# Scores of two attention stages: three split fp32r products against one plain fp32 product

## What is computed

```python
def _L0_xattn_ref(x, y, ...):                       # first layer
    xn = layernorm(x, ln1_w, ln1_b)
    yn = layernorm(y, ln2_w, ln2_b)
    q = (xn @ Wq), k, v = (yn @ Wkv)                # split into 16 heads of 16
    attn = jax.nn.softmax(jnp.einsum('bhqd,bhkd->bhqk', q, k) * scale, axis=-1)
    o = jnp.einsum('bhqk,bhkd->bhqd', attn, v).transpose(0, 2, 1, 3).reshape(B, N1, C1)
    x = x + (o @ Wproj + bproj)
    h = jax.nn.gelu(layernorm(x, ln3_w, ln3_b) @ W1 + b1, approximate=False)
    return x + (h @ W2 + b2)

def _L1_xattn_ref(x, encoder_out, norm_w, wq, wkv, wout):   # second layer
    xn = x * jax.lax.rsqrt(jnp.mean(x * x, axis=-1, keepdims=True) + EPS_RMS) * norm_w
    q, k, v = ...                                   # q and k turned by rope, then scaled to length 1 per head
    logits = jnp.einsum('bqhd,bkhd->bhqk', q, k) * scale
    out = jnp.einsum('bhqk,bkhd->bqhd', jax.nn.softmax(logits, axis=-1), v)
    return residual + out @ wout
```

## Time and profile before

| what | us |
|---|---|
| time before, median of 3 runs | 385.97 |
| lowest and highest of them | 385.35, 391.71 |
| the profiled execution: its span | 386.9 |
| its own time apart from the span | not given |
| TensorE busy, share | 356.5, 92% |
| VectorE busy, share | 294.4, 76% |
| ScalarE busy, share | 239.3, 62% |
| GpSimd busy, share | 197.1, 51% |

### The profile page before, as it was taken

The page is one execution under the profiler, slowest core; times in us unless marked ns, Lnnn a source line. Parts: engine busy times, 40 slices in busy tenths (PEclk is TensorE's granted clock), DMA queues, the critical chain, the costliest instruction groups (busy, mean ns, idle before and its releaser), DMA issues.

```text
span 386.9 us, 11499 instructions
## 1 busy us (share of the span) xinstructions
PE 356.5 (92%) x4475; PEld 318.7 (82%) x4475; DVE 294.4 (76%) x654; ACT 239.3 (62%) x464; POOL 197.1 (51%) x177
## 2 busy tenths in 40 slices
PE   8998999999999989898999999978889989989974
PEld 5977888888888867798999998978778878878854
DVE  4799987989899773267755559467899999999752
ACT  2356677666677655815644476163877777777862
POOL 2474544554665611003331233248899998999810
PEclk9999999999999999999999999999999999999999
DMA  6853001110000000000000000000001001010001
GB/s 157 246 158 121 27 25 43 32 28 25 2 3 4 22 2 2 2 2 0 0 0 0 0 0 3 10 22 0 22 12 36 26 26 42 29 37 14 29 30 41
DMA packets 14432, 12.39 MB, mean 32 GB/s; under 512 B 2996, under 2 KB 13752, under 8 KB 14392
## 3 DMA queue, kind: packets, MB, share of 16 engines
q1 hardware_dynamic: 14384, 11.83, 10.4%
q10 hardware_dynamic: 8, 0.00, 0.0%
HBM read 9.73 MB, written 2.10 MB: 31 GB/s over the span
## 4 chain that ended last, share of the span: by engine, by line
PE 58%; issue 22%; DVE 10%; ACT 5%; POOL 4%; POOLq 0%; DVEq 0%; ACTq 0%
PE bank_qk L697 9%; PE banks_s L745 6%; PE bank_y L834 4%; PE bank_y L828 3%; PE banks_s L1032 3%; PE bank_t L800 3%; PE bank_qk L722 3%; PE bank_o L736 3%; PE bank_t L697 3%; PE bank_qk L726 3%; DVE row_max L1203 2%; POOL x_all L375 2%; PE bank_y L1052 2%; PE bank_o L1021 2%; PE bank_y L929 1%
## 5 line engine op out<-in xcount | busy, mean ns | idle before, releaser
L413 POOL TENSOR_TENSOR norm_inv<-norm_sq_min,minus_half 128x32 f32<-128x32 f32 x16 | 87.5, 5468 | 1.8 <-DVE norm_sq_min L1374 1.8
L576 ACT ACTIVATE W_s<-banks_s,b_cols 128x256 f32<-128x256 f32 x60 | 25.0, 469 | 41.3 <-PE banks_s L915 41.3
L342 POOL TENSOR_TENSOR masked<-qkT_r,halves_t 128x512 fp32r<-128x512 f32 x32 | 32.9, 1050 | 24.1 <-DVE qkT_r L1193 24.1
L477 ACT ACTIVATE PT<-banks_s 128x1024 f32<-128x1024 f32 x32 | 31.0, 1022 | 20.3 <-PE banks_s L782 18.3
L1203 DVE TENSOR_REDUCE row_max<-banks_s 128x8 f32<-128x1024 f32 x32 | 37.6, 1218 | 7.7 <-PE banks_s L745 7.7
L368 POOL TENSOR_TENSOR b_var_eps<-b_mean_var,eps_t 128x2 f32<-128x2 f32 x8 | 1.6, 197 | 69.1 <-DVE b_mean_var L1137 69.1
L915 PE MATMUL banks_s<-lnT_hi,W_hi 128*128 128x256 f32 x120 | 34.2, 285 | 0.0
L915 PE MATMUL banks_s<-lnT_hi,W_lo 128*128 128x256 f32 x120 | 33.9, 283 | 0.0
L915 PE MATMUL banks_s<-lnT_lo,W_hi 128*128 128x256 f32 x120 | 33.9, 283 | 0.0
L642 ACT ACTIVATE PT<-banks_s 128x1024 f32<-128x1024 f32 x32 | 31.1, 1024 | 4.1 <-PE banks_s L1032 4.1
L745 PE MATMUL banks_s<-masked,qkT_r 32*128 32x256 f32 x768 | 31.5, 294 | 1.6 <-DVE row_max L1203 1.3
(11 more groups left out here) (171 smaller groups left out, 1095.6 us busy)
## 6 DMA issues: line engine op xcount, KB each, us to landing
ctx_in<-in_ctx SPq DMA_DIRECT2D x32, 96.0 KB, 2.0
x_all<-in_x SPq DMA_DIRECT2D x16, 128.0 KB, 2.1
W_s<-in_L_xattn_W SPq DMA_DIRECT2D x2, 1024.0 KB, 6.4
out<-Wq_s SPq DMA_DIRECT2D x16, 128.0 KB, 1.8
Wq_s<-in_L_xattn_Wq SPq DMA_DIRECT2D x1, 256.0 KB, 3.0
Wkv_s<-in_L_xattn_Wkv SPq DMA_DIRECT2D x1, 256.0 KB, 3.2
Wproj_s<-in_L_xattn_Wproj SPq DMA_DIRECT2D x1, 256.0 KB, 4.2
wout_s<-in_L_xattn_wout SPq DMA_DIRECT2D x1, 256.0 KB, 3.0
```

The source lines that it names most:

```text
L342: nc.gpsimd.tensor_tensor(masked[:, r, 1, :, half, :], qkT_r[:, r, 1, :, :].bitcast(fp32), ones, ALU.mult)\
L413: nc.gpsimd.tensor_tensor(norm_inv[:, j, :], norm_sq_min[:, j, :], minus_half[:, :], ALU.pow)\
L477: nc.scalar.activation(PT[:, 2 * h:2 * h + 2, :], banks_s[:, 2 * h:2 * h + 2, :], ACT.Exp, scale=HD ** -0.5)\
L576: last = nc.scalar.activation(hT[:, m, :], (bank or bank_s[u])[:, 256 * k:256 * k + 256], ACT.Gelu, bias=b1_cols[:, m:m + 1])
```

## The change

The score products of both attentions become plain fp32 matmuls of unsplit operands: 8 products a set in place of 24. `qkT_r` becomes `qkT` (fp32, no high and low), `masked` loses its axis of 2 too.

In stage A ScalarE copies the queries and keys once (`queries_keys_T`, the former L446), its `masked_hi` goes, VectorE's `queries_keys_lo` goes, and GpSimd makes the two masked copies from ScalarE's copy (`masked_pool`), in the place of `masked_lo`. In stage C ScalarE's three copies stay (`units_out`, now fp32), and VectorE's `units_lo` goes. What waited for VectorE's low parts now waits for ScalarE's copies. The projections, the products with `picks_wide` and those of stages B and C (`split_mm`) stay as they are.

```diff
-        qkT_r = sb("qkT_r", 128, RING, 2, 4, TOK, dtype=fp32r)
-        masked = sb("masked", 128, RING, 2, 4, 2, TOK, dtype=fp32r)
-        pair = masked[:, :, :, 0:KT, :, :]
+        qkT = sb("qkT", 128, RING, 4, TOK)
+        masked = sb("masked", 128, RING, 4, 2, TOK)
+        pair = masked[:, :, 0:KT, :, :]
...
-            def masked_lo(t):
+            def masked_pool(t):
 
                 if ok(t):
                     r = t % RING
-                    pool.wait_ge(a_qk_lo, t + 1)
+                    pool.wait_ge(a_qk_ready, t + 1)
                     wait(pool, a_shifted, t - 2)
                     for half in range(2):
                         ones = halves_t[:, half:half + 1].unsqueeze(2).broadcast_to([128, 4, TOK])
-                        nc.gpsimd.tensor_tensor(masked[:, r, 1, :, half, :], qkT_r[:, r, 1, :, :].bitcast(fp32), ones, ALU.mult)\
-                            .then_inc(a_masked_lo, 1)
+                        nc.gpsimd.tensor_tensor(masked[:, r, :, half, :], qkT[:, r, :, :], ones, ALU.mult).then_inc(a_masked_pool, 1)
...
-            def queries_keys_hi(t):
+            def queries_keys_T(t):
 
                 if ok(t):
                     act.wait_ge(A["qk_mm"], t + 1)
                     wait(act, a_shifted, t - 2)
-                    nc.scalar.activation(qkT_r[:, t % RING, 0, :, :], bank_qk[:, :].rearrange("p (a b) -> p a b", a=4), ACT.Copy)\
-                        .then_inc(a_qk_hi, 1)
-
-            def masked_hi(t):
-
-                if ok(t):
-                    act.wait_ge(a_qk_hi, t + 1)
-                    for half in range(2):
-                        nc.scalar.activation(masked[:, t % RING, 0, :, half, :], qkT_r[:, t % RING, 0, :, :].bitcast(fp32),
-                                             ACT.Copy, scale=halves_t[:, half:half + 1]).then_inc(a_masked_hi, 1)
...
                 exps_a(s - 4)
-                queries_keys_hi(s - 1)
+                queries_keys_T(s - 1)
                 on_T(s - 5)
-                masked_hi(s - 1)
                 out_T(s - 4)
...
-            def units_hi(t, j):
+            def units_out(t, j):
 
                 if ok(t):
                     act.wait_ge(c_turned, t + 1)
                     wait(act, C["scores"], NG * (t - 1))
                     for half in range(2):
-                        nc.scalar.activation(pair[:, j, 0, :, half, :], bank_o[:, 0:C1].rearrange("p (a b) -> p a b", a=KT),
-                                             ACT.Copy, scale=halves_t[:, half:half + 1]).then_inc(c_unit_hi, 1)
-                    nc.scalar.activation(qkT_r[:, j, 0, KT:, :], bank_o[:, C1:].rearrange("p (a b) -> p a b", a=KT), ACT.Copy)\
-                        .then_inc(c_unit_hi, 1)
+                        nc.scalar.activation(pair[:, j, :, half, :], bank_o[:, 0:C1].rearrange("p (a b) -> p a b", a=KT),
+                                             ACT.Copy, scale=halves_t[:, half:half + 1]).then_inc(c_unit_T, 1)
+                    nc.scalar.activation(qkT[:, j, KT:, :], bank_o[:, C1:].rearrange("p (a b) -> p a b", a=KT), ACT.Copy)\
+                        .then_inc(c_unit_T, 1)
...
-                    for n, (a, b) in enumerate(HI_LO):
-                        for g in range(QUARTERS):
-                            last = mm(bank_s[g][:, 2 * TOK * tile:2 * TOK * (tile + 1)], qkT_r[quad(g), r, a, rows + tile, :],
-                                      masked[quad(g), r, b, columns + tile, :, :], start=n == 0 and (stop or tile == 0), stop=stop and n == 2)
-                            if stop and tile == KT - 1 and n == 2:
-                                last.then_inc(A["scores"], 1)
+                    for g in range(QUARTERS):
+                        last = mm(bank_s[g][:, 2 * TOK * tile:2 * TOK * (tile + 1)], qkT[quad(g), r, rows + tile, :],
+                                  masked[quad(g), r, columns + tile, :, :], start=stop or tile == 0, stop=stop)
+                        if stop and tile == KT - 1:
+                            last.then_inc(A["scores"], 1)
 
             def scores_a(t):
 
                 if ok(t):
-                    pe.wait_ge(a_masked_hi, 2 * t + 2)
-                    pe.wait_ge(a_masked_lo, 2 * t + 2)
+                    pe.wait_ge(a_masked_pool, 2 * t + 2)
...
-                    wait(pe, c_unit_lo, t)
+                    wait(pe, c_unit_T, 3 * t)
...
-                    pe.wait_ge(c_unit_lo, t + 1)
+                    pe.wait_ge(c_unit_T, 3 * t + 3)
                     wait(pe, C["exped"], 2 * t)
                     for half in range(KT):
-                        for n, (k, q) in enumerate(HI_LO):
-                            for g in range(NG):
-                                last = mm(bank_s[g][:, 2 * TOK * half:2 * TOK * (half + 1)], qkT_r[quad(g), j, k, KT + half, :],
-                                          pair[quad(g), j, q, half, :, :], start=n == 0, stop=n == 2)
-                                if half == KT - 1 and n == 2:
-                                    last.then_inc(C["scores"], 1)
+                        for g in range(NG):
+                            last = mm(bank_s[g][:, 2 * TOK * half:2 * TOK * (half + 1)], qkT[quad(g), j, KT + half, :],
+                                      pair[quad(g), j, half, :, :], start=True, stop=True)
+                            if half == KT - 1:
+                                last.then_inc(C["scores"], 1)
...
-                    pe.wait_ge(c_unit_lo, upto(t + 3))
+                    pe.wait_ge(c_unit_T, 3 * upto(t + 3))
...
-            def queries_keys_lo(t):
-
-                if ok(t):
-                    r = t % RING
-                    dve.wait_ge(a_qk_hi, t + 1)
-                    v.tensor_tensor(qkT_r[:, r, 1, :, :], bank_qk[:, :].rearrange("p (a b) -> p a b", a=4),
-                                    qkT_r[:, r, 0, :, :].bitcast(fp32), ALU.subtract).then_inc(a_qk_lo, 1)
...
                 norm(s)
-                queries_keys_lo(s - 1)
                 maxima(s - 2)
...
-            def units_lo(t, j):
-
-                if ok(t):
-                    dve.wait_ge(c_unit_hi, 3 * t + 3)
-                    for half in range(2):
-                        v.scalar_tensor_tensor(pair[:, j, 1, :, half, :], bank_o[:, 0:C1].rearrange("p (a b) -> p a b", a=KT),
-                                               halves_t[:, half:half + 1], pair[:, j, 0, :, half, :].bitcast(fp32),
-                                               ALU.mult, ALU.subtract)
-                    v.tensor_tensor(qkT_r[:, j, 1, KT:, :], bank_o[:, C1:].rearrange("p (a b) -> p a b", a=KT),
-                                    qkT_r[:, j, 0, KT:, :].bitcast(fp32), ALU.subtract).then_inc(c_unit_lo, 1)
...
                 turned(s - 1, 1 - j)
-                units_lo(s - 3, 1 - j)
                 square_sums(s - 1, 1 - j)
```

More of the change, by code:

```diff
@@ L201, in build @@
         A, C = att_sems("a"), att_sems("c")
-        a_centred, a_qk_hi, a_qk_lo, a_masked_hi, a_masked_lo = (
-            sem(f"a_{k}") for k in ("centred", "qk_hi", "qk_lo", "masked_hi", "masked_lo"))
+        a_centred, a_qk_ready, a_masked_pool = (sem(f"a_{k}") for k in ("centred", "qk_ready", "masked_pool"))
         a_maxed, a_max_hi, a_max_lo, a_max_turned, a_maxT, a_shifted = (
@@ L208, in build @@
         c_stored = [sem(f"c_stored{j}") for j in range(2)]
-        c_rope, c_turned, c_rot, c_rot_sq, c_norm_sq, c_norm_min, c_norm_inv, c_unit, c_unit_hi, c_unit_lo = (
-            sem(f"c_{k}") for k in ("rope", "turned", "rot", "rot_sq", "norm_sq", "norm_min", "norm_inv", "unit", "unit_hi", "unit_lo"))
+        c_rope, c_turned, c_rot, c_rot_sq, c_norm_sq, c_norm_min, c_norm_inv, c_unit, c_unit_T = (
+            sem(f"c_{k}") for k in ("rope", "turned", "rot", "rot_sq", "norm_sq", "norm_min", "norm_inv", "unit", "unit_T"))
         b_stats_raw, b_stats, b_var, b_rstd, b_norm, b_bias, b_T, b_lnT_hi, b_lnT_lo, b_w1, b_gelu, b_hT_hi, b_hT_lo, b_w2, b_x, b_raw, b_centred = (
@@ L347, in step_a @@
                 residual_bias(s)
-                masked_lo(s - 1)
+                masked_pool(s - 1)
             pool.wait_ge(const_ready, 2)
@@ L355, in _ @@
             inverse_std(2)
-            masked_lo(0)
+            masked_pool(0)
             residual_bias(1)
@@ L359, in _ @@
             inverse_std(3)
-            masked_lo(1)
+            masked_pool(1)
             residual_bias(3)
-            masked_lo(2)
+            masked_pool(2)
             inverse_std(4)
             residual_bias(4)
-            masked_lo(3)
+            masked_pool(3)
             def inverse_std_b(p):
@@ L445, in queries_keys_hi @@
                     wait(act, a_shifted, t - 2)
-                    nc.scalar.activation(qkT_r[:, t % RING, 0, :, :], bank_qk[:, :].rearrange("p (a b) -> p a b", a=4), ACT.Copy)\
-                        .then_inc(a_qk_hi, 1)
-            def masked_hi(t):
-                if ok(t):
-                    act.wait_ge(a_qk_hi, t + 1)
-                    for half in range(2):
```

(28 more changed lines are left out.)

## The result

The changed kernel took 394.51 us (391.67 to 395.81, four runs) against 387.32 us (385.35 to 391.71, four runs) for the kernel before: a ratio of 1.0202, 95% interval 1.0135 to 1.027. With the same program run again (first experiment) the ratio is 1.0124 (1.0061 to 1.0188). It is slower, by one to two per cent; the forecast was 1.1%. The ratios leave out executions more than 1.5% above the fastest of the same kernel, so they are not the quotients of the medians shown. Experiment 1 shows what the two ratios have in them besides the change.

A forecast was written before the change was run, and what follows sets the result against it. TensorE was taken to bound the steady part of both attention stages. Opening -0.7, first stage +3.9, passage -0.35, second stage +1.65, end -0.2 sum to +4.3 us: forecast 390.3 us, 1.1% slower, range 385 to 397 us.

The forecast's parts named there:

- A burst: Score products on TensorE, both attention stages: 1.07 us for a set instead of 0.92, 0.15 us more.
- edge: Part of each score burst outside its rounds (first weights, draining): 0.20 us, the same before and after.
- Bursts on the path: Score bursts that lengthen the run: 26 in the first attention stage, +3.9 us; 11 in the steady second, +1.65 us.
- The passage: Into the second attention stage, where VectorE's low parts leave the chain: 0.35 us gained, from 0 to 0.5.
- The end: Last two score bursts of the second stage: a 0.25 us wait goes, each burst 0.15 longer, -0.2 us together.
- the opening: 13 to 40.5 us, VectorE on the path: without its low-part subtraction, work comes sooner, -0.7 us including five bursts.
- the move costs nothing: First stage: GpSimd's two masked products start one step sooner, their result wanted some 6 us later, so no cost.
- The base: Starting time: the profiled 386.9 us span taken as 0.9 us above the run median 385.97, turning 391.2 into 390.3.
- two abreast: Rival: product halves run in program order, 2.14 us a burst, +1.22 on 39 bursts, about 436 us; chance 0.07.
- staggered loads: Rival: weight loads of 128 columns stagger the strips, +0.48 us a burst on 39 bursts, about 404 us; chance 0.08.
- single streaming: Rival: a 32-row strip pays no second streaming, burst 0.68 us, about 374 us, faster; chance 0.04.
- More relief than counted: Rival: freed VectorE and ScalarE time is worth more, in second-stage tiles and opening, about 386 us; chance 0.06.

The follow-up runs named there:

- first experiment: The changed kernel with no edit, timed in more rounds beside the kernel before: 394.01 us (six runs), ratio 1.0124.
- Experiment 1: The same as the first experiment: the changed kernel again with no edit, more rounds: 394.01 us (six runs), ratio 1.0124.
- run 5: The changed kernel with score loops swapped in both attention stages, so each strip's products follow one another in the program: 397.14 us, one run.
- run 3: The kernel before with plain fp32 score products in the second attention stage alone: 387.04 us, ratio 0.9987.
- run 2: The changed kernel, but the second attention stage keeps the split products and VectorE's low parts: 392.66 us, ratio 1.0084.
- run 4: The changed kernel, but GpSimd's masked copies of tile 2 wait until VectorE has normalised tile 3: 393.42 us, ratio 1.0105.
- run 8: The changed kernel, but ScalarE makes both masked copies of the first stage and GpSimd none: 391.23 us (four runs), ratio 1.0117.
- run 6: The changed kernel with each score product of the second stage made twice into the same bank: 403.84 us, one run.
- runs 5 and 7: 7: the kernel before with only the high x high product in second-stage scores, VectorE still making low parts: 387.81 us, one run.

## Why the prediction was right, and where it was not

The forecast was slower by 4.3 us, within 2%; it is 5.14 us from the first burst on. Step by step:

- **A burst.** Forecast 1.07 us, 16 instructions of 0.216 us in four rounds and 0.20 us of edge; the chain has 1.07 to 1.08, and 1.94 when doubled. Reading four abreast from the starts of L800 was right, and program order falls with run 5. The mean of one is 400 ns, not near 380. The trace has the four first ones of a burst at 478 ns, each starting together with its own weight load, and the other twelve at 374. The starts also show what the edge is: rounds start at 0, 0.32, 0.54 and 0.75 us and the next line at 1.07, so the first and the last step are 0.10 us longer each. The split bursts have the same 0.10 us twice.
- **Bursts on the path.** Forecast 26 in the first stage, +3.9; +4.01. In the second 11, +1.65; ten tiles gave +1.60 and the eleventh burst 0.16 more. Tiles of 8.6 and 7.4 us: 8.65 and 7.44.
- **The passage.** -0.35 forecast, -0.33 measured. The chain there:

```profile
274.52 0.64 ACT rot_sq L601
275.19 0.70 DVE norm_sq L1341
...
276.00 0.70 DVE inT_r L1317
```

The 1.1 us of L1389 and L1392 are gone, and ScalarE's squares end last in their place, which is why only a third of it came back. From x_all the passage is the same in run 3 (4.95 us) and untouched in run 2 (5.28).
- **The end.** -0.2 forecast for the last two bursts; the stretch from burst 13 gave -0.36, with +0.16 for the thirteenth burst in it, so about -0.5. The waits of 0.25 us went, as said, but TensorE's turn of the values, which waited, went from 0.41 to 0.22 us too, and that I had not counted. The kernel before has, behind the wait of 0.25 us at 368.53,

```profile
368.78 0.41 PE bank_o L1062 x2
369.19 1.01 PE banks_s L1032 x23
```

and the changed kernel

```profile
374.21 0.91 PE bank_qk L682 x6
375.12 0.22 PE bank_o L1044 x2
375.34 1.20 PE banks_s L1014 x16
```

Each time 0.44 us goes and the burst is 0.19 longer: -0.5 for two.
- **The step that went wrong: the opening.** "The third maxima and the work up to 40.5 us come 0.7 us sooner." It came 0.25 us later. The relief that I summed was there: run 4, which only removes the collision, has -0.54. What I left out is in my sentence that GpSimd's products start one step sooner and "the move costs nothing". I asked only who waits for their result, not whom they run beside. Taking L1193 out took away the wait that kept GpSimd apart from VectorE's L1185. In the steady part such collisions are hidden under TensorE: L1167 takes about 1.2 us four times more there, the same product is long more often in run 8, beside other work of GpSimd, and yet the stretch from burst 6 to x_all is 228.10 to 228.15 us in both and in runs 1 and 4. In the opening VectorE is the path. This is worth 0.79 of the 0.84 us by which the sum was too low; the rest of the opening (0.16), the first stage (0.11), the second (0.09) and the end (-0.31) nearly cancel.
- **The base.** I took the profiled execution of the kernel before as 0.9 us above the median because its span is. But a time is longer than its span, in the kernel before by 1.7 to 1.8 us (388.7 and 386.9), so that execution was 2.7 us above the median shown. The median of 29 runs is 388.7; with 5.14 that makes 393.8, and 394.0 was measured. That this fits so well is partly luck, since 388.7 is merely the middle one of three groups. Of the 3.7 us by which the forecast of 390.3 lies below 394.0, 0.84 is the sum and the rest mostly this.

Of the rivals, two abreast (1.07 us instead of 2.14) and staggered loads (instead of 1.40) fall with the burst, and so does single streaming (instead of 0.68), with run 6 besides. More relief than counted happened at the end alone, 0.3 us.

## What to carry to other kernels

On an engine that bounds a stage, compare what a burst lasts, not how many instructions it has: 16 plain fp32 instructions last longer than 24 fp32r ones, and less work on engines with room to spare does not pay for that. When an edit takes a wait away, ask not only who gets the result sooner, but what the freed instruction now runs beside, above all where the other engine is on the path. And compare kernels from a common event on (here the first score burst), which told 0.1 us apart where medians of 4 to 29 runs left a whole per cent open, and look at the granted clock of every stretch that you compare.

## What the runs showed of the hardware

- The start differs by up to 4 us between executions: 26 products of a fixed size take 3.06 us in one execution of the changed kernel and 5.33 in another, 4.41 in the profile of the kernel before. They step by 0.213 us until TensorE's granted clock is on record at its upper level (at 4.33 to 13.51 us in ten traces) and by 0.109 us from then on. From the first burst on, two executions of one program agreed to 0.01 us in all and to 0.02 us in each stretch.
- In runs 5 and 7 the granted clock was at its lower level for 3.4 us within the MLP stage, which cost 1.5 us on code that was not edited.
- A VectorE product with two inputs from SBUF took 1.19 instead of 0.41 us beside a GpSimd product, and the GpSimd pair 2.34 instead of 2.04; beside VectorE's row maxima out of a PSUM bank GpSimd kept its 2.04 us.
- Plain fp32 products on four strips of 32 rows run abreast however they are ordered: 1.07 us tile by tile, 1.10 us strip by strip.
